# Rotary layer: the convolution taps move from the preparation into the attention loop on VectorE, GpSimd subtracts half of the row maxima, and the values are projected once and turned

## The reference

```python
q = x @ wq.T + bq
k = (x @ wk.T + bk) * scaling
v = x @ wv.T + bv
lepe = conv_general_dilated(v, lepe_w, padding 2, 5x5, one filter per channel) + lepe_b
qr, kr = theta_shift(qh, sin, cos), theta_shift(kh, sin, cos)      # per head, 12 heads of 16
qk = einsum('bnld,bnmd->bnlm', qr, kr) + mask                      # 1024 x 1024 per head
out = einsum('bnlm,bnmd->bnld', softmax(qk), vr)
out = (out, heads side by side) + lepe
return out @ wo.T + bo
```

## Time and profile before

| what | value |
|---|---|
| median of three runs | 8046.31 us (8032.21 to 8073.91) |
| the profiled execution: span from first to last instruction | 8043.7 us |
| TensorE busy over the span | 7011.3 us, 87% |
| VectorE busy | 4978.2 us, 62% |
| ScalarE busy | 3803.5 us, 47% |
| GpSimd busy | 2019.4 us, 25% |
| mean granted TensorE clock | 0.908 of full speed |
| rotary preparation | 5577.36 to 6250.60 us, 673 us |
| rotary attention | 6250.60 us to the end, 1793 us |

### The profile page before, as it was taken

One profiled execution on the slowest core, in us unless ns is written; L12 is line 12 of the kernel. 1 busy time (PEld: TensorE's weight loads), 2 busy tenths in 40 slices (PEclk: granted clock), 3 DMA queues, 4 the chain that ended last, 5 costly groups with the idle time before them and its releaser, 6 DMA issues. The chain is left out here.

```text
span 8043.7 us, 157230 instructions
## 1 busy us (share of the span) xinstructions
PE 7011.3 (87%) x56704; PEld 4290.7 (53%) x56704; DVE 4978.2 (62%) x7151; ACT 3803.5 (47%) x7049; POOL 2019.4 (25%) x2407
## 2 busy tenths in 40 slices
PE   3999999999877899469999999997776799999999
PEld 2555555555555556345555555553332466666665
DVE  4555555555555666445555555554888577777776
ACT  0444444444522555224444444443111577777777
POOL 3344344334220000043443443441111000000000
PEclk7999999999988989779999999998766899999999
DMA  7776776776459756477667667664222555455453
GB/s 160 154 140 122 139 136 117 138 140 122 88 178 216 133 110 122 103 163 141 124 129 142 126 124 140 133 123 96 77 72 72 138 124 136 121 130 130 120 135 88
DMA packets 500587, 1025.92 MB, mean 128 GB/s; under 512 B 80391, under 2 KB 276680, under 8 KB 460568
## 3 DMA queue, kind: packets, MB, share of 16 engines
q1 hardware_dynamic: 452694, 932.07, 53.5%
q0 software_dynamic: 47360, 86.53, 6.6%
HBM read 670.94 MB, written 358.93 MB: 128 GB/s over the span
## 5 line engine op out<-in xcount | busy, mean ns | idle before, releaser
L1512 DVE TENSOR_REDUCE a_nmp<-a_S 128x2 f32<-128x1024 f32 x1536 | 1878.8, 1224 | 1153.3 <-PE a_S L1357 1139.9
L1616 ACT ACTIVATE a_PROB<-a_T 128x512 f32<-128x512 f32 x3072 | 1667.7, 595 | 1750.0 <-PE a_T L1336 1742.5
L1215 POOL CAST a_RF<-a_RL 32x512 fp32r<-32x512 f32 x1536 | 1297.7, 845 | 1138.5 <-DVE a_RL L1540 1046.6
L2397 DVE CUSTOM_DVE_ANT_0 a_X<-a_S,a_mask 128x1024 f32<-128x1024 f32 x768 | 916.9, 1222 | 466.0 <-PE a_S L2293 462.3
L2440 ACT ACTIVATE a_PROB<-a_T 128x512 f32<-128x512 f32 x1536 | 836.3, 602 | 291.6 <-PE a_T L2307 291.6
L1332 PE MATMUL a_T<-a_QW,a_KW 64*128 64x512 f32 x3072 | 799.5, 513 | 181.1 <-ACT a_PROB L1616 108.2
L1332 PEld LDWEIGHTS a_T<-a_QW,a_KW 64*128 64x128 f32 x3072 | 309.5, 190 | 1161.0 <-issue 1157.9
L1370 PE MATMUL a_O<-a_PROB,a_V 128*32 128x512 f32 x6144 | 898.8, 660 | 2.5 <-ACT a_PROB L1616 2.5
L2307 PE MATMUL a_T<-a_ident,a_X 128*128 128x128 f32 x6144 | 827.4, 278 | 3.7
L2307 PEld LDWEIGHTS a_T<-a_ident,a_X 128*128 128x128 f32 x6144 | 671.2, 141 | 201.3 <-issue 183.1
L1357 PEld LDWEIGHTS a_S<-a_KV,a_QV 64*128 64x128 f32 x6144 | 650.2, 199 | 120.8
(11 more groups left out here) (178 smaller groups left out, 9248.2 us busy)
## 6 DMA issues: line engine op xcount, KB each, us to landing
a_QV<-a_part_rows SPq DMA_DIRECT2D x384, 256.0 KB, 7.7
a_rel_rows<-a_RF SPq DMA_DIRECT2D x96, 1024.0 KB, 9.2
a_K<-part_rows SPq DMA_DIRECT2D x576, 128.0 KB, 4.1
a_part_rows<-a_part SPq DMA_DIRECT2D x48, 1024.0 KB, 16.9
a_QV<-a_part_rows SPq DMA_DIRECT2D x384, 128.0 KB, 8.2
a_QV<-a_rel_rows SPq DMA_DIRECT2D x384, 128.0 KB, 7.9
a_QW<-a_rel_rows SPq DMA_DIRECT2D x192, 256.0 KB, 9.9
a_mask<-L_mask SPq DMA_DIRECT2D x48, 1024.0 KB, 8.6
```

Source lines behind the costliest of these rows:

```text
L1215: nc.gpsimd.tensor_copy(dst, src).then_inc(permuted, 1)
L1512: nc.vector.tensor_reduce(nmp[:, qh, c, 2 * pr:2 * pr + 2, kh], S[:, pr], AX.X, ALU.max).then_inc(s_done, 1)
L1616: nc.scalar.activation(PROB[:, s % PRING, 2 * pr + sd], T[:, slot(("st", s, pr, sd))], ACT.Exp).then_inc(t_act, 1)
L2397: nc.vector.tensor_tensor_reduce(out=X[:, v % 2, c, g], in0=S[:, sd].rearrange("p a b -> p (a b)"), in1=mask[:, n % 2, g, c], scale=1.0, s ...
```

## The change

The change is in the rotary layer alone.

- The values are projected once, by channel, for a pair of images together (`by_channel`: two images' 64 channels in the upper and lower half of a tile). ScalarE puts them with their bias into `VC` and into the padded image `VP`. TensorE turns `VC` (`by_token`, 4 transposes a tile). The padded images go to memory as `pad_rows`.
- Of the convolution, the preparation keeps only the first quarter of the rows of the first channel group: 25 taps of 256 elements a pair, 100 in all. The other 44 quarters, of 25 taps of 256 elements each, are done in the attention loop, 25 taps over two units, 3 or 4 taps behind each `row_max` (`convolve`). SyncE loads each padded piece from `pad_rows` (`padded`, three buffers), GpSimd stores each result to `lepe_rows` (`convolved`), SyncE loads a unit's piece of it into `LP` (`lepe`, 4 DMAs), and VectorE adds it to the attention's output before the projection with `wo` (`add_lepe`). The separate projection of the convolution, its bias and its adding store are gone.
- The subtraction of the maximum from the first tile of each pair moves from VectorE to GpSimd (`lower`).
- The semaphores of the layers before are cleared and used again, with one more meeting of all engines ahead of the rotary layer. The copy of the input into the output is issued image by image.

```diff
+    TURNS = (("vc", 0, 0), ("vc", 0, 1), ("vc", 1, 0), ("vt", 0, 0), ("vc", 1, 1), ("vt", 0, 1),
+             ("vc", 2, 0), ("vt", 1, 0), ("vc", 2, 1), ("vt", 1, 1), ("vt", 2, 0), ("vt", 2, 1))
+
+    def turns(b, i):
+        return [(n, b // 2, g, t) for n, g, t in TURNS[2 * i:2 * i + 2]] if b % 2 else []
...
+                sp.dma_start(stream_out[b], x_in[b]).then_inc(copied, 16)
...
+                if odd:
+                    sp.wait_ge(t_act, TALLY[("vt", p, GROUPS - 1, 1)])
+                    alone(sp)
+                    for g in range(GROUPS):
+                        sp.dma_start(pad_rows[g, p], VP[:, p % 2, g].rearrange("p y x -> p (y x)")).then_inc(pad_stored, 16)
+                    for o in range(2):
+                        sp.dma_start(v_rows[2 * p + o], VT[:, o]).then_inc(v_stored, 16)
+                    sp.wait_ge(taps, N_TAPS * (p + 1))
+                    alone(sp)
+                    sp.dma_start(lepe_rows[0, p], CV[:, p % 2]).then_inc(cv_stored, 16)
...
+            def by_channel(p, g, t):
+                n = ("vc", p, g, t)
                 free(n)
                 alone(pe)
+                for k in range(2):
+                    for odd in range(2):
+                        last = nc.tensor.matmul(T[64 * odd:64 * odd + 64, slot(n)], wv[:, k, 64 * g:64 * g + 64],
+                                                XN[:, (2 * p + odd) % HELD, k, t * BANK:(t + 1) * BANK],
+                                                start=k == 0, stop=k == 1)
                 last.then_inc(t_ready, 1)
+            def by_token(p, g, t):
+                n = ("vt", p, g, t)
                 free(n)
+                pe.wait_ge(t_act, TALLY[("vc", p, g, t)])
                 alone(pe)
+                for c in range(4):
+                    last = nc.tensor.transpose(T[:, slot(n), P * c:P * c + P], VC[:, (2 * g + t) % 3, P * c:P * c + P],
+                                               ident_sb[:])
                 last.then_inc(t_ready, 1)
...
-                src = VP[:, p % 2, j, dy:dy + SIDE, dx:dx + SIDE]
-                dst = CV[:, p % 2, j].rearrange("p (a b) -> p a b", a=SIDE)
+                src = VP[:, p % 2, 0, dy:dy + QUARTER, dx:dx + SIDE]
+                dst = CV[:, p % 2].rearrange("p (a b) -> p a b", a=QUARTER)
...
+                    if b % 2 and i >= FIRST_TAPS:
+                        j, of = i - FIRST_TAPS, PIECES - FIRST_TAPS
+                        for k in range(N_TAPS * j // of, N_TAPS * (j + 1) // of):
+                            tap(b // 2, k)
...
+                nc.scalar.activation(VC[:, (2 * g + t) % 3], T[:, slot(n)], ACT.Identity, bias=bv[:, g:g + 1])
+                nc.scalar.activation(VP[:, p % 2, g, 2 + 16 * t:18 + 16 * t, 2:2 + SIDE],
                                      T[:, slot(n)].rearrange("p (y x) -> p y x", x=SIDE),
-                                     ACT.Identity, bias=bv[:, j:j + 1]).then_inc(t_act, 1)
...
+    FIRST, CONVS, PADS = PAIRS_N, QUARTERS * PAIRS_N, 3
...
+            def padded(j):
+                (hg, qq), p = divmod(j // PAIRS_N, 4), j % PAIRS_N
+                need(sp, accumulated, N_TAPS * (j - FIRST - PADS + 1))
+                alone(sp)
+                at = PAD * QUARTER * qq
+                sp.dma_start(VP[:, j % PADS].rearrange("p y x -> p (y x)"), pad_rows[hg, p][:, at:at + PAD * ROWS_P]
+                             ).then_inc(pad_loaded[j % PADS], 16)
+
+            def lepe(v):
+                n, b = divmod(v, IMAGES)
+                j, odd = PAIRS_N * n + b // 2, b % 2
+                if j >= FIRST:
+                    sp.wait_ge(conv_stored[j % 2], 16 * ((j - FIRST) // 2 + 1))
+                if v < 2:
+                    sp.wait_ge(lp_cleared, 1)
+                alone(sp)
+                for g in range(G):
+                    at = 64 * odd + DIM * g
+                    sp.dma_start(LP[Q * g:Q * g + DIM, v % 2], lepe_rows[n, b // 2, at:at + DIM]).then_inc(lp_loaded[v % 2], 16)
...
+            for j in range(FIRST, FIRST + PADS):
+                padded(j)
+            for v in range(2, UNITS + 2):
                 if v < UNITS:
                     operands(v)
-                values(v - 1)
+                if v <= UNITS:
+                    values(v - 1)
+                lepe(v - 2)
                 n, b = divmod(v, IMAGES)
                 if b >= 4 and n + 1 < QUARTERS:
                     masks(n + 1, b - 4)
+                j = FIRST + PADS + v // 2 - 1
+                if v % 2 == 0 and j < CONVS:
+                    padded(j)
...
+            def lower(v, nth):
+                c, p = SCORES[nth]
+                pool.wait_ge(s_done, TILES_U * v + 2 * nth + 1)
+                here = X[:, v % 2, c, 2 * p]
+                nc.gpsimd.tensor_scalar(here, here, rmax[:, v % 2, c, 2 * p:2 * p + 1], -1.0, ALU.subtract, ALU.mult
+                                        ).then_inc(x_pool, 1)
+
+            def convolved(j):
+                pool.wait_ge(accumulated, N_TAPS * (j - FIRST + 1))
+                alone(pool)
+                pool.dma_start(lepe_rows[j // PAIRS_N, j % PAIRS_N], CV[:, j % 2]).then_inc(conv_stored[j % 2], 16)
+
+            for u in range(UNITS + 1):
+                for nth in range(G):
+                    if u + 1 < UNITS:
+                        lower(u + 1, nth)
+                    if u and nth == 2:
+                        store(u - 1)
+                if u % 2 and FIRST + u // 2 < CONVS:
+                    convolved(FIRST + u // 2)
...
-                    pe.wait_ge(x_dve, G * u + 2 * (p + 1))
+                    pe.wait_ge(x_pool, G * u + 2 * (p + 1))
...
-                    pe.wait_ge(t_dve, upto(u, "turn", "dve"))
+                    pe.wait_ge(lepe_added, u)
...
-                    if sd == 0 and between is not None:
-                        divide(between)
-                eng.wait_ge(s_done, i + 1)
-                here = X[:, v % 2, c, 2 * p]
-                nc.vector.tensor_scalar(here, here, rmax[:, v % 2, c, 2 * p:2 * p + 1], -1.0, ALU.subtract, ALU.mult
-                                        ).then_inc(x_dve, 1)
+                    if between is not None:
+                        (add_lepe if sd else divide)(between)
+
+            def tap(j, k):
+                dy, dx = divmod(k, TAPS)
+                hg = j // PAIRS_N // 4
+                src = VP[:, j % PADS, dy:dy + QUARTER, dx:dx + SIDE]
+                dst = CV[:, j % 2].rearrange("p (y x) -> p y x", x=SIDE)
+                if k == 0:
+                    eng.wait_ge(pad_loaded[j % PADS], 16 * ((j - FIRST) // PADS + 1))
+                    need(eng, conv_stored[j % 2], 16 * ((j - FIRST) // 2))
+                    alone(eng)
+                    ins = nc.vector.tensor_scalar(dst, src, lw[:, hg, 0:1], lb[:, hg:hg + 1], ALU.mult, ALU.add)
+                else:
+                    eng.wait_ge(accumulated, N_TAPS * (j - FIRST) + k)
+                    ins = nc.vector.scalar_tensor_tensor(out=dst, in0=src, scalar=lw[:, hg, k:k + 1], in1=dst,
+                                                         op0=ALU.mult, op1=ALU.add)
+                ins.then_inc(accumulated, 1)
+
+            def convolve(u, nth):
+                j, at = FIRST + u // 2, G * (u % 2) + nth
+                if j < CONVS:
+                    for k in range(N_TAPS * at // (2 * G), N_TAPS * (at + 1) // (2 * G)):
+                        tap(j, k)
 
...
+            def add_lepe(v):
+                eng.wait_ge(t_dve, upto(v + 1, "turn", "dve"))
+                eng.wait_ge(lp_loaded[v % 2], 16 * G * (v // 2 + 1))
+                alone(eng)
+                nc.vector.tensor_tensor(OSB[:], OSB[:], LP[:, v % 2], ALU.add).then_inc(lepe_added, 1)
...
+                convolve(u, 0)
                 if u:
                     invert(u - 1)
                 if u + 1 < UNITS:
                     row_max(u + 1, *SCORES[1], between=u - 1 if u else None)
                 else:
                     divide(u - 1)
-                if u + 1 < UNITS:
-                    row_max(u + 1, *SCORES[2])
-                    row_max(u + 1, *SCORES[3])
+                    add_lepe(u - 1)
+                convolve(u, 1)
+                for nth in range(2, G):
+                    if u + 1 < UNITS:
+                        row_max(u + 1, *SCORES[nth])
+                    convolve(u, nth)
...
+            sems.pop_all()
+            nc.clear_and_free_semaphores(nc.allocated_since(before))
+            nc.all_engine_barrier()
```

More of the change, by code:

```diff
@@ L1797, in _ @@
             sp.dma_start(X[:, 1], x_in[1]).then_inc(x_loaded[1], 16)
-            sp.wait_ge(consts_loaded, CONSTS)
-            alone(sp)
             for b in range(IMAGES):
-                sp.dma_start(stream_out[b], x_in[b]).then_inc(consts_loaded, 16)
-            for b in range(IMAGES):
+                p, odd = divmod(b, 2)
                 if b + 2 < IMAGES:
@@ L1874, in mean @@
                                  start=True, stop=True).then_inc(averaged, 1)
-            def padded(p, j, t):
```

(63 more changed lines are left out.)

210 lines of the change are left out of this document (84 added, 126 removed).

## The result

The changed kernel takes **8294.32 us** (median of 4 runs, 8287.51 to 8301.78), the kernel before 8047.07 us beside it (4 runs, 8032.21 to 8073.91). The ratio is 1.030, with a 95% interval of 1.0278 to 1.0322. The forecast was 8262 us, slower. The profiled execution has a span of 8300.1 us, 256.4 us over the 8043.7 us of before.

The account below looks back on a forecast made before the run. VectorE was taken to set the preparation's pace, TensorE to be nearly full in the attention. 8043.7 - 344 + 457 + 103 = 8260 us, 8262 us against the median; range for 8 in 10: 8100 to 8410.

Parts of the forecast that it names:

- preparation: Stage before the attention: 673 us shrinks to 329 us (289 to 399), a gain of 344 us.
- the wait: stall and clock: SyncE's queue in even steps: 41 stalls waiting for taps, 457 us, plus 103 us of TensorE at half speed.
- GpSimd's subtraction: Attention loop: 1.2 us each (1.2 to 3.1), done when the taps begin, so priced at zero.
- The mechanism of the wait: SyncE's queue: operands of the next unit stand behind the wait for taps, so TensorE stalls in every even body.
- the other signs: Profile after: last 12 or so units again 18.2 us, preparation near 330 us with TensorE over 80% busy, among others.
- The stall: Start of even bodies: TensorE waits 11.1 us (9.5 to 12.5) for taps, operand issues and landing.
- The clock: TensorE behind each stall: half speed loses 2.5 us (1 to 4), 103 us in 41 stalls.
- rival 2: Attention: a 3.1 us GpSimd subtraction holds taps and VectorE becomes the bound, 287 us more, about 8550; chance 0.07.
- rivals 3 and 4: Preparation: memory or TensorE's clock limits the gain to 200 us, or its time stays; 8406 us; chance 0.05.
- rival 1: Even bodies: stall costs less than the preparation gives; chance 0.07 near 8050, 0.07 near 7700 if the wait is covered.

Follow-up runs that it names:

- e5: e1 with the subtraction of pair 3 moved from GpSimd back to VectorE: 7691.52 us, ratio 0.954 to the kernel before.
- e1: Changed kernel, each padded piece loaded one even step later in SyncE's queue, so its wait is for earlier taps: 7788.19 us, ratio 0.967 to the kernel before.
- e2: Kernel before plus only a SyncE wait in 41 even steps for the running unit's pair 3 row maximum: 8496.14 us, ratio 1.055.
- e8: Changed kernel with the wait for the same taps moved to the following odd step, behind the operands: 8038.69 us, ratio 0.997 to the kernel before.
- e7: e1 with GpSimd's subtraction written as one operation on two tensors: 7745.94 us (1 run).

## Why the prediction was right, and which terms were off

The result is what the sum had, a gain and a loss, and one loss more that the sum had at zero. The last column is how each was measured.

| term | predicted | measured | by |
|---|---|---|---|
| preparation | -344 | -373 | profile: 299.9 - 673.2; by medians, e5 against before: 7692 - 8065 = -373 |
| the wait: stall and clock | +457 +103 | +506 | after against e1; by units 41 x (50.94 - 2 x 19.04) = 527 |
| GpSimd's subtraction | 0 | +97 | e1 against e5; by units 81 |
| sum | +216 | +230 | after against before, in the medians used above: 8294 - 8065; against before's runs beside it: 8294 - 8047 = +247 |

The three medians add up by construction, since e5 and e1 stand between before and after. What checks them is the profile. The preparation's 373.3 us are read there directly. From its end to the last instruction the time is 1793.1 us before, 1798.6 in e5, 1885.4 in e1 and 2407.0 after: 5.5 us are neither term, 86.8 are the subtraction and 521.7 the wait. That e5 and the profile give the same 373 for the preparation is in part chance: in the two profiled executions e5 is only 351 us under before, 19 us by what lies ahead of the preparation.

**The mechanism of the wait was right.** SyncE's long waits are the 41 on the taps, the stall stands in front of pair 0 in every second body, the body behind it has none, the attention's clock is 0.87, under the 0.95 that I had named, and it comes back when the taps end (0.99). Of the other signs two missed: the last units take 19.0 us and not 18.2, by the subtraction, and TensorE is busy for 79% of the preparation and not over 80%. e2 makes the same loss in the kernel before, e1 takes it out of the kernel after, and e8 changes what it hits. I count this as shown.

**The stall: 11.1 predicted, 11.3 measured.** TensorE's idle time is 11.8 us on the mean ((529.0 - 43.9 for the layer's first wait) / 41), but 0.54 us of it is the wait on the row maximum that was there before. What was too small is the four taps, 2.04 us against 1.7: a tap follows the one before after 0.51 us, not 0.43. The slope had been read from operations that mostly didn't depend on each other. In the stall shown the last `K` also landed some tenths later than 4.0 us after its issue; the mean stall is shorter than that one. (The lower end of 9.5 us was 0.3 too low by its own figures: 11.1 - (4.0 - 2.7) is 9.8.)

**The clock: 2.5 predicted, 1.6 measured** (50.94 - 2 x 19.04 - 11.29). The half-speed stretch is there (1.22 for 0.73 us, 3.57 us for 16 transposes where 8 take 1.09). e2 lost 2.03 us by it, where TensorE fills the unit. In the kernel after GpSimd sets a part of the unit, and so probably covers some of it; no run tried that apart. I had taken the price of a full TensorE and at the same time left out what made it less full.

**The step that failed: the price of GpSimd's subtraction.** I had the ends 1.2 and 3.1 us and took the lower "since this has one tensor input". The runs gave 3.72 us, above both. The one-input row that I went by the earlier trace rows is a cast, with no arithmetic by a value per partition. That row couldn't price a subtraction and a multiplication in one pass; which of the two things, the second operation or the value per partition, makes this form slow no run here shows. By the other reading (rival 2), 3 us would have made VectorE the bound and cost 287 us. That didn't come either: this form doesn't hold the taps (485 ns beside it in e1, 483 in e5, with fewer of them). What it did instead is plainer. GpSimd finishes late, and TensorE's transposes wait 0.8 us for it, once a unit in e1 and in the units without a stall in the kernel after (52 waits, 42.8 us). e7 has the holding that I had described, with an operation of two tensors. One of my readings was loose as well: the L2033 operation of 0.73 us in the earlier trace rows ended before GpSimd's addition began (6118.74 against 6118.91), so it shows nothing of the two side by side. Three others of the kernel before did lie beside such an addition, and took 0.75 us.

Here the Trainium skill's rule ("GPSIMD Engine Reference", 8. Key points: contention with VectorE instructions of two SBUF inputs) is borne out by e7 (taps 0.63 us in place of 0.49, on the mean), but not, for the taps, by the form that the change uses. And the estimate of 0.9 us from the same page (3.1, 1.03 cycles an element at 1.2 GHz) is a quarter of the 3.72 us measured. The measurements decide.

**The preparation: -344 predicted, -373 measured.** TensorE is busy 238 us at clock 0.89 and VectorE 220 us, above my 219 and 197. But the two lie beside each other better than I had it: I had added 16 us for turns and 40 us for half clock to 219, and 30 us for the last stores and the block's end; of the 276 us behind the start only 38 are over TensorE's busy time, for all of it. The halves of the array do overlap, 1.81 us a tile of 8 matmuls of 512 columns (I had 1.72; the first row below has two tiles), and the 24 us at the start are the normalisation beside GpSimd's memsets as before:
```profile
5645.81 3.65 PE L1880 MATMUL n_T<-n_XN,n_wv 96*64 96x512 f32 x16
...
5604.04 12.87 DVE L1941 TENSOR_SCALAR n_XN<-n_X,n_gm,n_rstd 96x1024 f32<-96x1024 f32 x2 [0.98 <-POOL n_rstd L1829]
5607.16 5.21 POOL L1835 MEMSET n_VT<- 128x6144 f32 x1
```
Memory wasn't the bound: 202 GB/s at a DMA share of 0.54. With that rivals 3 and 4 are out.

**Two errors met.** The loss by the wait was too large by 54 us, GpSimd's 97 us were missing, and the gain was too small by 29 us. The forecast is 32 us under the measured time, nearer than its terms are: they are 14 us short together, and 18 us are the kernel before, which has 8065 us in the later runs and 8047 in the first. The nearness is luck in part, the size of the wait's term is not. The 7700 us that rival 1 gave to a wait that costs nothing is what e5 measures, once the subtraction is out of the way too.

## What to carry to other kernels

A wait in a queue that is served in order costs what is queued behind it, not how long it lasts. SyncE waits 979 us on the taps in the slow kernel, and 719 us in e8, at half of the cost; the question is which transfer leaves late and who needs it first. When work is moved to an engine that is idle, price it by an instruction of the same form, or move so little (one pair of four) that a factor of three does no harm. And when two kernels differ in several things, close the account: here e5 and e1 stand 373 and 277 us under the kernel before and the kernel after 230 us over it, and each step between them has its own edit. Such differences always add up, so each needs a second measure, here the length of a unit and of a stage in the profile.

## What the hardware showed that I had not expected

- **GpSimd, 128x1024 float32.** Subtract and multiply with one value per partition takes 3.72 us, the subtraction of two tensors, one of them a repeated column, 1.89 us.
- **What each does to VectorE.** Beside the 3.7 us form, taps keep 0.485 us, but the copy of 128x256 (`inverse_wide`) has a mean of 847 ns in e1 against 294 in e5 and e7, where it falls into gaps. One of 1.26 us began at 7031.74 in e1 and ended 0.2 us after the subtraction that GpSimd had begun at 7029.07. Beside the 1.9 us form the taps are the ones that are held.
- **Dependent taps.** Those of 128x256 on VectorE follow each other every 0.51 us; with 485 ns for one, hardly anything overlaps.
- **TensorE's clock** fell to the lower level behind each of the 41 stalls of 2.3 to 4.6 us in e8 as behind those of 12 us, and by the granted clock it was back 3.4 to 6.7 us after the matmuls began again in e2, and 4.5 to 10.1 us after it in e8. In e8 it fell in 23 of the 41 stalls only after they had begun again, up to 1.9 us later. That cost 2.03 us a stall in e2, where TensorE sets the pace, and 1.6 in the kernel after, where it doesn't alone.
